# Experts: finding a token's four by comparing with the fourth largest masked score

## The reference

```python
s = sigmoid(x @ router_w.T) + bias            # 16 per token
group_score = top_k(s.reshape(-1, 4, 4), 2)[0].sum(-1)
gidx = top_k(group_score, 2)[1]               # two of four groups stay
masked = where(emask, s, -1.0)
topk_idx = top_k(masked, 4)[1]                # four experts; of equal ones the first
tw = take_along_axis(scores, topk_idx, axis=1)
tw = tw / (tw.sum(-1, keepdims=True) + 1e-20) * 2.5
routed = sum over the four of tw * (silu(x @ gate) * (x @ up)) @ down
```

## Time and profile before

| | |
|---|---|
| median of three runs | 2253.85 us |
| the profiled execution | 2246.64 us |
| its span, first to last instruction | 2244.8 us |
| PE busy | 2005.9 us (89%) |
| DVE busy | 1696.5 us (76%) |
| ACT busy | 1060.5 us (47%) |
| POOL busy | 518.5 us (23%) |
| mean granted clock of TensorE | 0.959 of full |

### The profile page before, as it was taken

One profiled execution on the slowest core, in us unless ns is written; L12 is line 12 of the kernel. 1 busy time (PEld: TensorE's weight loads), 2 busy tenths in 40 slices (PEclk: granted clock), 3 DMA queues, 4 the chain that ended last, 5 costly groups with the idle time before them and its releaser, 6 DMA issues. The chain is left out here.

```text
span 2244.8 us, 53059 instructions
## 1 busy us (share of the span) xinstructions
PE 2005.9 (89%) x19268; PEld 1549.8 (69%) x19268; DVE 1696.5 (76%) x4490; ACT 1060.5 (47%) x2084; POOL 518.5 (23%) x536
## 2 busy tenths in 40 slices
PE   5999995687769999996999997976999999999998
PEld 3666664566646666664666665755888888888887
DVE  4777775777736888885888885666888888888886
ACT  3666653455444555553555553433444444444443
POOL 1111110000001223221222222653322322232231
PEclk9999997999978999997999998997999999999999
DMA  3000000000000000001100001000000000000000
GB/s 123 29 19 27 28 10 1 1 1 0 0 1 2 0 0 0 0 0 29 30 28 28 28 10 64 0 0 1 6 11 5 5 5 10 5 5 10 5 5 10
DMA packets 27248, 30.41 MB, mean 14 GB/s; under 512 B 1936, under 2 KB 20624, under 8 KB 26896
## 3 DMA queue, kind: packets, MB, share of 16 engines
q1 hardware_dynamic: 27152, 29.28, 4.2%
HBM read 25.08 MB, written 4.19 MB: 13 GB/s over the span
## 5 line engine op out<-in xcount | busy, mean ns | idle before, releaser
L429 DVE TENSOR_REDUCE mx<-ps 128x8 f32<-128x512 f32 x384 | 261.9, 682 | 170.3 <-PE ps L574 169.9
L338 ACT ACTIVATE ex<-ps 128x512 f32<-128x512 f32 x384 | 230.1, 599 | 265.0 <-PE ps L592 263.2
L1111 ACT ACTIVATE moe_sg<-ps 128x512 f32<-128x512 f32 x288 | 172.5, 599 | 365.2 <-PE ps L1163 365.0
L1147 PEld LDWEIGHTS ps<-down,moe_act 128*128 128x128 f32 x2048 | 266.0, 191 | 33.0 <-DVE moe_acc L1340 12.6
L592 PE MATMUL ps<-pack,sh 128*128 128x128 f32 x1536 | 249.4, 285 | 32.1 <-DVE sh L431 31.5
L1147 PE MATMUL ps<-down,moe_act 128*128 128x128 f32 x2048 | 271.4, 275 | 5.8 <-DVE moe_acc L1340 5.8
L431 DVE TENSOR_TENSOR sh<-ps,mx 128x512 f32<-128x512 f32 x384 | 265.4, 691 | 13.2
L608 PEld LDWEIGHTS ps<-vblk,ex 128*64 128x64 f32 x6144 | 212.5, 139 | 64.6 <-issue 64.4
L608 PE MATMUL ps<-vblk,ex 128*64 128x32 f32 x6144 | 255.3, 226 | 0.0
L592 PEld LDWEIGHTS ps<-pack,sh 128*128 128x128 f32 x1536 | 168.2, 142 | 125.3 <-issue 65.2
L1322 DVE TENSOR_TENSOR moe_act<-ps,moe_sg 128x512 f32<-128x512 f32 x288 | 197.3, 685 | 68.2 <-PE ps L1163 55.6
(11 more groups left out here) (234 smaller groups left out, 3529.3 us busy)
## 6 DMA issues: line engine op xcount, KB each, us to landing
ctxT<-in_ctx SPq DMA_DIRECT2D x32, 256.0 KB, 2.8
x_res<-in_x SPq DMA_DIRECT2D x16, 256.0 KB, 2.9
kmi<-in_key_mask SPq DMA_DIRECT2D x16, 256.0 KB, 3.4
out<-moe_acc SPq DMA_DIRECT2D x16, 256.0 KB, 2.3
pack<-in_pack SPq DMA_DIRECT2D x1, 2536.5 KB, 9.4
wqkv<-in_wqkv SPq DMA_DIRECT2D x1, 1536.0 KB, 8.3
gate<-in_gate SPq DMA_DIRECT2D x6, 192.0 KB, 4.0
up<-in_up SPq DMA_DIRECT2D x6, 192.0 KB, 4.1
```

The costliest lines, as they stand in the source:

```text
L338: nc.scalar.activation(ex[:, u % 2], UB[u % 4].rearrange("p (c n) -> p c n", n=P), ACT.Exp).then_inc(e_ready, 1)
L429: nc.vector.tensor_reduce(mx[:, u % 2], sc, AX.X, ALU.max).then_inc(max_done, 1)
L1147: last = nc.tensor.matmul(YB[k % 2][:, t * D:(t + 1) * D], act_[:, k % 3, t * P:(t + 1) * P], down[:, k, :], start=True, stop=True)
```

## The change

The ranking is replaced. MAX8 gives each token's eight largest masked scores, of which the fourth is the level. What is above it is taken; of those equal to it, the first ones are taken until there are four: the number above plus a running count of equal ones (a scan that starts again at each token) must be at most 4. All of it is on DVE; `rank_experts` is gone from POOL. In the array of constants `lowmask` (256 columns) gives way to `ereset` (64). The wait count `NR` goes from 29 to 32, and the sum `wsum` moves from part 6 to part 7.

```diff
-        NR = 29
+        NR = 32
...
-            def rank_experts(g):
-                pool.wait_ge(routing, before(g, 21))
-                nc.gpsimd.tensor_tensor(by_tile(eeq), by_tile(eeq), C["lowmask"]..., ALU.mult).then_inc(routing, 1)
-                pool.wait_ge(routing, before(g, 22))
-                nc.gpsimd.tensor_tensor(by_tile(egt), by_tile(egt), by_tile(eeq), ALU.add).then_inc(routing, 1)
...
+                fourth = top8[:, :, 3].unsqueeze(2).broadcast_to((P, TILES, E))
...
                     dve.wait_ge(routing, before(g, 19))
-                    V.tensor_tensor(egt[:, :, :, :], all_others(masked), one_by_one(masked), ALU.is_gt).then_inc(routing, 1)
+                    dve.sem_inc(passed, 1)
+                    for n in range(TILES):
+                        last = V.max(top8[:, n, :], masked[:, n * E:(n + 1) * E])
+                    last.then_inc(routing, 1)
                 if 5 in parts:
-                    V.tensor_tensor(eeq[:, :, :, :], all_others(masked), one_by_one(masked), ALU.is_equal).then_inc(routing, 1)
+                    V.tensor_tensor(t16(above), t16(masked), fourth, ALU.is_gt).then_inc(routing, 1)
+                    V.tensor_tensor(t16(level), t16(masked), fourth, ALU.is_equal).then_inc(routing, 1)
+                    V.tensor_reduce(nabove[:, :], t16(above), AX.X, ALU.add).then_inc(routing, 1)
+                    V.tensor_tensor_scan(nlevel[:, :], C["ereset"], level[:, :], 0.0, ALU.mult, ALU.add).then_inc(routing, 1)
                 if 6 in parts:
-                    V.tensor_reduce(rank[:, :], egt[:, :, :, :].rearrange("p t e j -> p (t e) j"), AX.X, ALU.add).then_inc(routing, 1)
-                    V.scalar_tensor_tensor(w[:, :], rank[:, :], 4.0, score[:, :], ALU.is_lt, ALU.mult).then_inc(routing, 1)
-                    V.tensor_reduce(wsum[:, :], t16(w), AX.X, ALU.add).then_inc(routing, 1)
+                    V.tensor_tensor(t16(place), t16(nlevel), nabove[:, :].unsqueeze(2).broadcast_to((P, TILES, E)), ALU.add).then_inc(routing, 1)
+                    V.scalar_tensor_tensor(tied[:, :], place[:, :], 4.0, level[:, :], ALU.is_le, ALU.mult).then_inc(routing, 1)
+                    V.tensor_tensor(taken[:, :], tied[:, :], above[:, :], ALU.add).then_inc(routing, 1)
+                    V.tensor_tensor(w[:, :], taken[:, :], score[:, :], ALU.mult).then_inc(routing, 1)
                 if 7 in parts:
+                    V.tensor_reduce(wsum[:, :], t16(w), AX.X, ALU.add).then_inc(routing, 1)
```

More of the change, by code:

```diff
@@ L39 @@
                ("ff1", 4 * D), ("ff1b", 4), ("ff2", 4 * D), ("router", 16), ("rbias", 64),
-               ("lowmask", 256), ("glowmask", 16), ("ident4", 2 * S)]:
+               ("ereset", 64), ("glowmask", 16), ("ident4", 2 * S)]:
     COLS[_n] = (_at, _w)
@@ L932, in experts_phase @@
         masked = sb("masked", [P, TE])
-        egt = sb("egt", [P, TILES, E, E])
-        eeq = sb("eeq", [P, TILES, E, E])
-        rank = sb("rank", [P, TE])
+        top8 = sb("top8", [P, TILES, 8])
+        above = sb("above", [P, TE])
+        level = sb("level", [P, TE])
+        nabove = sb("nabove", [P, TILES])
+        nlevel = sb("nlevel", [P, TE])
+        place = sb("place", [P, TE])
+        tied = sb("tied", [P, TE])
+        taken = sb("taken", [P, TE])
         w = sb("w", [P, TE])
@@ L971, in experts_phase @@
         stored = [sem(f"stored{s}_") for s in (0, 1)]
[L973 to L980, removed]
         def before(g, n):
@@ L1015, in low_rows @@
                 nc.gpsimd.tensor_tensor(x_lo[:, s], xnT[:, s], x_hi[:, s], ALU.subtract).then_inc(x_split, 1)
-            def rank_experts(g):
-                pool.wait_ge(routing, before(g, 21))
-                nc.gpsimd.tensor_tensor(by_tile(eeq), by_tile(eeq), C["lowmask"].unsqueeze(1).broadcast_to((P, TILES, E * E)), ALU.mult).then_inc(routing, 1)
-                pool.wait_ge(routing, before(g, 22))
-                nc.gpsimd.tensor_tensor(by_tile(egt), by_tile(egt), by_tile(eeq), ALU.add).then_inc(routing, 1)
             def split_weights():
@@ L1047, in first_prep @@
                 split_weights()
-                rank_experts(g)
             def step(g, s, first, more):
@@ L1059, in step @@
                 add_part(g, 1)
-                if more:
-                    rank_experts(g + 1)
                 add_part(g, 2)
@@ new lines, in route @@
+                    dve.wait_ge(routing, before(g, 21))
+                    V.tensor_tensor(t16(level), t16(masked), fourth, ALU.is_equal).then_inc(routing, 1)
+                    dve.wait_ge(routing, before(g, 22))
+                    V.tensor_reduce(nabove[:, :], t16(above), AX.X, ALU.add).then_inc(routing, 1)
+                    dve.wait_ge(routing, before(g, 23))
+                    V.tensor_tensor_scan(nlevel[:, :], C["ereset"], level[:, :], 0.0, ALU.mult, ALU.add
+                                         ).then_inc(routing, 1)
@@ L1288, in route @@
                 if 6 in parts:
-                    dve.wait_ge(routing, before(g, 23))
-                    V.tensor_reduce(rank[:, :], egt[:, :, :, :].rearrange("p t e j -> p (t e) j"), AX.X,
+                    dve.wait_ge(routing, before(g, 24))
+                    V.tensor_tensor(t16(place), t16(nlevel), nabove[:, :].unsqueeze(2).broadcast_to((P, TILES, E)),
                                     ALU.add).then_inc(routing, 1)
-                    dve.wait_ge(routing, before(g, 24))
-                    V.scalar_tensor_tensor(w[:, :], rank[:, :], 4.0, score[:, :], ALU.is_lt,
+                    dve.wait_ge(routing, before(g, 25))
@@ L1295, in route @@
+                    V.scalar_tensor_tensor(tied[:, :], place[:, :], 4.0, level[:, :], ALU.is_le,
                                            ALU.mult).then_inc(routing, 1)
-                    dve.wait_ge(routing, before(g, 25))
+                    dve.wait_ge(routing, before(g, 26))
+                    V.tensor_tensor(taken[:, :], tied[:, :], above[:, :], ALU.add).then_inc(routing, 1)
+                    dve.wait_ge(routing, before(g, 27))
+                    V.tensor_tensor(w[:, :], taken[:, :], score[:, :], ALU.mult).then_inc(routing, 1)
@@ L1297, in route @@
+                if 7 in parts:
+                    dve.wait_ge(routing, before(g, 28))
                     V.tensor_reduce(wsum[:, :], t16(w), AX.X, ALU.add).then_inc(routing, 1)
-                if 7 in parts:
-                    dve.wait_ge(routing, before(g, 26))
+                    dve.wait_ge(routing, before(g, 29))
                     V.tensor_scalar(wsume[:, :], wsum[:, :], 1e-20, None, ALU.add).then_inc(routing, 1)
-                    dve.wait_ge(routing, before(g, 27))
+                    dve.wait_ge(routing, before(g, 30))
@@ L1302, in route @@
                     V.reciprocal(winv[:, :], wsume[:, :]).then_inc(routing, 1)
-                    dve.wait_ge(routing, before(g, 28))
+                    dve.wait_ge(routing, before(g, 31))
                     V.scalar_tensor_tensor(comb[:, s], t16(w), 2.5, winv[:, :].unsqueeze(2).broadcast_to((P, TILES, E)), ALU.mult,
@@ L2073 @@
     put("rbias", np.broadcast_to(np.tile(a["L1_ffn_bias"], TILES), (P, 64)))
-    put("lowmask", np.broadcast_to(np.tril(np.ones((16, 16)), -1).reshape(1, -1), (P, 256)))
+    put("ereset", np.broadcast_to(np.arange(64) % 16 > 0, (P, 64)))
     put("glowmask", np.broadcast_to(np.tril(np.ones((4, 4)), -1).reshape(1, -1), (P, 16)))
```

## The result

| | changed | before, beside it |
|---|---|---|
| median, lowest to highest, us | 2234.72 (2230.98 to 2250.02), 19 runs | 2251.58 (2247.54 to 2266.58), 19 runs |
| ratio, 95% interval | 0.9923 (0.9909 to 0.9937) | |
| profiled execution, its span, us | 2243.04, 2241.2 | 2246.64, 2244.8 |

A forecast was written before the change was run, and what follows sets the result against it. PE was taken as the bound, DVE close behind; start 5.6 + steady state 9.2 - moved addition 1.0 + load 0.3 = 14.1 us off 2246.64. Against the three-run median that gave 2239.7, stated as 2240 us, range 2230 to 2250.

The forecast's parts named there:

- Start, 5.9 us less 0.3: Last phase's start: group 0's shorter ranking chain lets PE restart 5.9 us earlier, less 0.3 for the clock: 5.6 us.
- The clock's term: PE's restart at half clock may last 4.33 us instead of 3.0: 0.3 us off, bounds 0 and 0.65.
- Steady state, 9.2 us: At k = 10 DVE accumulates expert 8 some 0.75 us earlier, so PE's down-product waits go: 9.2 us.
- Both kinds of wait: PE's waits for expert 8's accumulation, losing 0.49 and 0.75 us, seven groups each; both were to go.
- The moved addition, 1.0 us: POOL's second addition moves to k = 11 and may hold DVE's scan: 0 to 4.5 us lost, 1.0 taken.
- a lost tie: In part 5 POOL's addition starts before DVE's scan and holds it; PE waits 0.3 us at k = 14.
- The loop's end, 0: DVE's stand at its loop's top, six times, stays: 0, bound one more stand of 2.4 us x 6 below.
- The rival of a second stand: Top of DVE's loop: longer body runs out of fetched code once more per iteration, 2254 to 2268 us; chance 0.05.
- The load, 0.3: Constants shrink by 96 KB, so DVE's first use of them comes earlier: 0.3 us, bounds 0 and 0.34.
- Expected rows: Profile signs in the last phase: start wait about 11 us, `moe_acc` waits under 1, windows 42.4 and 44.1 us.
- the one that the addition hits everywhere: Rival: tie lost in all 15 groups and MAX8 as slow as on 64 elements: 2245 us; chance 0.17.
- the one that only the start gains: Rival: expert 8's accumulation stays late, leaving 5.9 us from start and load: 2248 us; chance 0.08.

The follow-up runs named there:

- The start alone: Changed kernel with the new selection only in group 0's routing, old ranking in the fifteen other groups, both constants loaded: ratio to before 0.9975, median 2252.72 us.
- the compare at k = 10: Changed kernel plus one 576-element DVE compare per group routed inside a step, right after the four MAX8: ratio to before 0.9973, median 2251.26 us.
- the run with POOL's reads: Changed kernel plus one 1024-element POOL operation per group, two operands in SBUF, released as the scan begins: ratio to before 0.9952, median 2246.12 us.

## Why the prediction came out right

Forecast 14.1 us off the profiled execution, 2240 us; measured 14.4 to 15.1 us between like profiles and 17.3 us (14.2 to 20.5) between medians, 2234.72 us. The absolute 2240 is 5.3 us off, 2.3 of it because the median of three runs before (2253.85) lay above that of 19 (2251.58). The steps:

- **Start, 5.9 us less 0.3.** Right: PE started again 5.83 us earlier, counted from `moe_xn` (the chain 2.95 us, forecast 2.9). The scan was 0.29 us, forecast 0.29 with a far end of 0.68; four MAX8 of 16 elements 0.41, forecast 0.47, plus 0.15 of idling before them that I hadn't counted. The clock's term was mis-sized: it took 0.65 back in the first profile and 1.1 in the second, not 0.3, for the lower level lasted 4.44 and 5.31 us. I had taken the middle of two rows (3.00 and 4.33) and the upper one for the bound; the second profile is beyond it. Net 5.2 and 4.7, forecast 5.6. The start alone gave 4.7.
- **Steady state, 9.2 us.** Right in mechanism and size: 9.5 us for 15 groups (9.8 by the second profiles). Both kinds of wait went, and the compare at k = 10 brought back 8.4 us of it.
- **The moved addition, 1.0 us.** Mis-sized: nothing. POOL started 0.32 us after the scan, in both kinds of group, where I had a tie within 0.1 us. POOL's side was right: counted from the group's start, ACT weighs expert 9 at 22.55 us (1920.58 - 1898.03), forecast 22.57 (1919.2 - 1896.63), and the addition starts at 23.77, forecast 23.77 (1920.4 - 1896.63). DVE's side was late in the forecast: I had expert 8's accumulation begin at 21.32 (1917.95 - 1896.63) and the scan at 23.82; they begin at 21.06 and 23.45. The price of a lost tie, 0.3 us, is not shown (see the run with POOL's reads). What the step didn't see is that `masked` is now held in every routing inside a step instead of every second one, in a place where it costs nothing.
- **The loop's end, 0.** Held: DVE stands 2.17 us (2.41 before), and PE's six waits of 1.3 us are as before. One more block of instructions is fetched in an iteration (six of 8 KB, not five), 1.2 us before the branch, without an effect. The rival of a second stand had its condition (a longer body) but not its place: the block was wanted in straight code.
- **The load, 0.3.** Mis-sized: DVE's first use of the constants stands at 10.08 and 10.13 us in the two profiles of before, at 10.07 where both constants are loaded, and at 9.48 to 9.81 in the eight with the smaller array: some 0.5 us, outside the bound of 0.34. That bound assumed time in proportion to bytes, and the load does not keep to it.
- **Expected rows.** Waits of PE at the start 11.4 (forecast 11), windows of 42.3 and 43.9 us (42.4 and 44.1), `moe_acc` at 0.4 us (under 1).

Against the forecast 14.1, by the first profiles, the start gave 0.4 less, the groups 0.3 more, the addition 1.0 more, the load 0.2 more, and the stretch after the last group start 0.4 that I had not forecast and have not traced: 15.6 us, of which 15.1 in the phase. By the second profiles the start gave 0.9 less and the groups 0.6 more. So the steps were right and the sum is close in part by luck, since the start and the other terms are off in opposite directions. No rival came true: the one that the addition hits everywhere resembles the run with POOL's reads, which keeps 10.2 us of the phase's gain; the one that only the start gains is what the run of the start alone shows, 4.7 us.

## What to carry to other kernels

Find out at which instruction the bound engine waits, and count only what the change removes ahead of it in the queue: 0.76 us there was worth 8.4 us over 15 groups and 0.6 us four products later. Add to a wait the start-up of the work behind it; the table of waits showed 5.8 us where 9.5 were to be had. And take two profiles of each kernel when the difference is below 1%, and compare the stretch that the change touches, not the spans.

## What the hardware showed beyond that

- **The early clock differs between executions of the same kernel.** PE's timeline, the same four matmuls in the changed kernel's first profile and in its second:

```profile
38.57 1.11 PE L592 MATMUL ps<-pack,sh 128*128 128x128 f32 x4
...
60.39 0.69 DVE L429 TENSOR_REDUCE mx<-ps 128x8 f32<-128x512 f32 x1 [3.37 <-PE ps L574]
```

```profile
38.40 0.66 PE L592 MATMUL ps<-pack,sh 128*128 128x128 f32 x4
...
51.81 0.69 DVE L429 TENSOR_REDUCE mx<-ps 128x8 f32<-128x512 f32 x1 [1.01 <-PE ps L574]
```

They take 1.11 and 0.66 us. In the first profile such a group takes 1.06 to 1.12 us up to 58 us and 0.66 only from 60.28 on; in the other from 38.40 on, and in the one of before from 38.70 on. The same `mx` on DVE, second row of each, is then 8.6 us later: most of the 11.5 us. The column of the granted clock reads 1.00 in both stretches, but the trace's first clock record, the full level, stands only at 59.1 us in the first profile and at 38.1 in the second (38.4 in the one of before), so the 1.00 ahead of it is no reading. Four matmuls of the same form take 1.11 us at 1527.99 too, where 0.50 is recorded. What makes the rise late is open.
- **A scan of 64 elements went from 0.29 to 1.83 us**, and a `tensor_scalar` of 4 elements from 0.17 to 1.00 us, beside a POOL operation that had started first. That an instruction with one operand in SBUF can be held too was not in my prediction, which called reduces and MAX8 safe for having one input and did not think of `tensor_scalar`; I haven't tested it apart.
- **A shorter pause did not mean a shorter restart.** After 16.8 and 16.9 us without matmuls PE ran at the level 0.50 for 2.9 and 3.0 us in the two profiles of before; after 10.9 to 11.4 us it did so for 4.4 to 5.6 us in the seven profiles of kernels with the new routing ahead of DVE's first product. Why is open.
- **Written-out code ran without a stand** in a phase where a loop of 447 instructions stood for 2.2 us at each return.
